# Four raw and four split buffers in place of six and three, in a split-precision adjacency matmul

## What is computed

```python
h = maximum(layernorm(x, axis=-1), 0.0)          # x: 8192 x 128, f32
x = x + (1.0 - 0.1) * (adj @ h) + 0.1 * h0       # adj: 8192 x 8192, f32; h0: 8192 x 128
```

## Time and profile before

| | |
|---|---|
| median of 3 runs | 709.2 us (709.12 to 709.41) |
| profiled execution, its own time | 709.23 us |
| its span in the trace | 707.4 us |
| PE busy | 702.4 us, 99% |
| DVE busy | 636.1 us, 90% |
| ACT busy | 531.6 us, 75% |
| bytes moved | 285.75 MB, mean 404 GB/s |
| chain that ended last | PE 99%, DMA 1% |

### The profile page before, as it was taken

How to read it: one execution, slowest core, us unless ns; L and a number is a source line. 1 busy time by engine, 2 the same in 40 slices (tenths; PEclk the granted TensorE clock), 3 DMA queues, 4 the chain that set the end, 5 groups by cost and what they waited for, 6 DMA issues and landing times.

```text
span 707.4 us, 8192 instructions
## 1 busy us (share of the span) xinstructions
PE 702.4 (99%) x3088; PEld 578.4 (82%) x3088; DVE 636.1 (90%) x567; ACT 531.6 (75%) x465; POOL 31.5 (4%) x38
## 2 busy tenths in 40 slices
PE   8999999999999999999999999999999999999998
PEld 5888888888888888888888888888888888888886
DVE  5999999999989999999998888888988898889885
ACT  5899988788788788778776767676767676767673
POOL 1101110000000000000000000000000000000000
PEclk9999999999999999999999999999999999999999
DMA  9999999999999999999999999999999999999990
GB/s 365 417 418 420 416 419 416 419 416 418 420 416 419 417 419 417 419 416 420 421 418 418 388 409 389 404 401 399 414 421 414 424 420 423 422 419 422 406 414 21
DMA packets 46551, 285.75 MB, mean 404 GB/s; under 512 B 5168, under 2 KB 9520, under 8 KB 14000
## 3 DMA queue, kind: packets, MB, share of 16 engines
q1 hardware_dynamic: 46080, 283.99, 98.0%
q10 hardware_dynamic: 432, 1.25, 0.5%
HBM read 281.02 MB, written 4.19 MB: 403 GB/s over the span
## 4 chain that ended last, share of the span: by engine, by line
PE 99%; DMA 1%; DVE 0%; SPq 0%; DVEq 0%; issue 0%
PE acc L478 16%; PE acc L473 16%; PE acc L474 16%; PE acc L462 16%; PE acc L451 16%; PE acc L457 16%; PE acc L420 1%; DMA raw<-early_dram 1%; PE acc L433 0%; PE acc L437 0%; PE acc L429 0%; DVE finished L368 0%; SPq L217 0%; DVEq L138 0%; DVEq L367 0%
## 5 line engine op out<-in xcount | busy, mean ns | idle before, releaser
L349 DVE TENSOR_TENSOR a_lo<-raw,a_hi 128x2048 fp32r<-128x2048 f32 (+2 forms) x310 | 585.4, 1907 | 55.7 <-ACT a_hi L305 54.8
L305 ACT ACTIVATE a_hi<-raw 128x2048 fp32r<-128x2048 f32 (+1 forms) x370 | 498.9, 1378 | 159.8 <-PE acc L478 100.1
L473 PE MATMUL acc<-a_hi,h_hi 128*128 128x512 f32 x512 | 199.2, 389 | 0.0
L474 PE MATMUL acc<-a_hi,h_lo 128*128 128x512 f32 x512 | 199.2, 389 | 0.0
L451 PE MATMUL acc<-a_hi,h_hi 128*128 128x512 f32 x504 | 167.5, 389 | 0.0
L457 PE MATMUL acc<-a_hi,h_lo 128*128 128x512 f32 x504 | 167.5, 389 | 0.0
L478 PE MATMUL acc<-a_lo,h_hi 128*128 128x512 f32 x512 | 136.8, 389 | 0.0
L462 PE MATMUL acc<-a_lo,h_hi 128*128 128x512 f32 x504 | 134.7, 389 | 0.0
L473 PEld LDWEIGHTS acc<-a_hi,h_hi 128*128 128x128 f32 x512 | 96.1, 188 | 20.0
L478 PEld LDWEIGHTS acc<-a_lo,h_hi 128*128 128x128 f32 x512 | 96.1, 188 | 20.0
L474 PEld LDWEIGHTS acc<-a_hi,h_lo 128*128 128x128 f32 x512 | 96.1, 188 | 19.9
(11 more groups left out here) (21 smaller groups left out, 31.5 us busy)
## 6 DMA issues: line engine op xcount, KB each, us to landing
raw<-tall_dram SPq DMA_DIRECT2D x128, 1024.0 KB, 8.3
raw<-wide_dram SPq DMA_DIRECT2D x126, 1024.0 KB, 11.8
res_sb<-res_dram SPq DMA_DIRECT2D x16, 512.0 KB, 10.2
x_sb<-x_dram SPq DMA_DIRECT2D x30, 128.0 KB, 11.9
out_dram<-finished SPq DMA_DIRECT2D x15, 256.0 KB, 8.6
raw<-early_dram ACTq DMA_DIRECT2D x2, 512.0 KB, 6.6
raw<-early_dram SPq DMA_DIRECT2D x2, 512.0 KB, 6.2
out_dram<-finished SPq DMA_DIRECT2D x2, 128.0 KB, 1.8
```

The source lines that it names most:

```text
L305: nc.scalar.activation(a_hi[:, q % SPLIT_SLOTS, cols], raw[:, q % RAW_SLOTS, cols], ACT.Copy).then_inc(hi_ready, 1)
L349: nc.vector.tensor_tensor(a_lo[:, q % SPLIT_SLOTS, cols], raw[:, q % RAW_SLOTS, cols], a_hi[:, q % SPLIT_SLOTS, cols].bitcast(fp32), ALU.s ...
L473: nc.tensor.matmul(bank, h_hi[:, k, :], a_hi[:, slot, cols], start=(k == 0), stop=False)
L474: nc.tensor.matmul(bank, h_lo[:, k, :], a_hi[:, slot, cols], start=False, stop=False)
```

## The change

One line: the raw slots go from six to four, and the split slots (a_hi and a_lo each) from three to four.

```diff
-RAW_SLOTS, SPLIT_SLOTS = 6, 3
+RAW_SLOTS, SPLIT_SLOTS = 4, 4
```

## The result

The changed kernel takes 758.2 us, the median of six runs from 752.7 to 765.9, against 709.3 us before. The ratio is 1.068, 95% interval 1.065 to 1.071. The runs of before lie within 0.4 us of each other; these spread over 13, and the ratio leaves out the longest, over 1.5% above the shortest. The forecast was 719 us with a range of 709 to 745. The profiled execution took 755.9 us, its span 754.1.

What follows compares the result with a forecast made beforehand. PE was taken to bound the kernel, its pace kept only if loads land within 6.6 us; 8.4 us in the wide stage and 1.7 late in the tall one, 10.1 on 709.23, gave 719 us, range 709 to 745.

Steps and rivals of the forecast that it cites:

- The bound and the loop of the raw slot: PE bounds at 2.72 us a piece; a slot goes through load, a_hi, a_lo, SP, with 4.3 us behind the landing.
- The landing: Load of a whole piece with no queue: about 5.5 us against 6.6 allowed, so the loop closes at 9.8 of 10.88.
- The terms of the sum: Wide stage from piece 44: 8.4 us; tall from 490 us: 1.7; before 116 us and tall to 490: 0.
- the lumps of DVE: Wide stage: DVE's other work delays issues by 1.0 or 1.6 us, idling DMA engines 0.44 us per four pieces.
- residual loads: They take 1.25 us each, 0.06 a unit in the wide stage, and leave little spare DMA rate late in the tall stage.
- the spread between the 16 engines: Wide stage: the slowest DMA engine decides the landing; raises the loss per four pieces from 0.3 to 0.4 us.
- Rival 2: The landing is long by itself, 7.8 us, loop 12.1 us, 786 us in all; chance 0.08 for anything above 745.
- the fourth split slot: Lets ACT run a piece further ahead, removes its 100.1 us of waits on PE; at most 0.2 us to gain.
- the moved stores: Stores move by two pieces in place but not in time, behind the same low_a: cost 0.
- the loads of x: At least 10.88 us lie between issue and statistics, against landings of 6 to 7 us: cost 0.
- The start: Piece 4 goes out at about 10 us instead of 3, its data due near 13: cost 0, at most 2 us.
- The range: 709 to 745 us, from rival 1's no loss to a shortest landing of 6.8 us; leaves out rivals 2 and 3.

Runs made afterwards that it cites:

- nores4: Changed kernel (four raw, four split slots) with only the first residual loaded and used for all chunks: 756.1 us, ratio 1.067.
- even13: Changed kernel with 13 matmuls a piece and an added SP wait, the load of piece q waiting for PE's piece q - 5: 771.4 us.
- p13: Kernel before (six raw, three split slots) with one matmul done twice in each piece, 13 matmuls: 766.5 us, one run.
- even4: Changed kernel, 12 matmuls a piece, with an added SP wait, the load of piece q waiting for PE's piece q - 5: 757.4 us, ratio 1.070.
- even12h: Changed kernel with a thirteenth matmul of 256 columns a piece and SP's added wait for PE's piece q - 5: 749.4, 751.5, 763.8 and 769.4 us.
- r4s3: Kernel before with four raw slots instead of six, split slots left at three: 757.5 us, ratio 1.068.
- p13r4: Changed kernel (four raw, four split slots) with one matmul done twice in each piece, 13 matmuls, no added wait: 768.6 us.
- r3s4: Changed kernel with three raw slots instead of four, four split slots: 837.4 us, one run.
- p13r4s3: Four raw and three split slots, against the changed kernel's four and four, with 13 matmuls a piece: 772.1 us, one run.
- p14: Kernel before (six raw, three split slots) with two matmuls done twice in each piece, 14 matmuls: 824.0 us, one run.
- two4: Changed kernel with each piece loaded as two halves of 512 KB, both issued only when the whole slot is free: 777.4 us, ratio 1.096.

## Why the prediction was wrong

- **The bound and the loop of the raw slot** were read rightly: PE at 99%, 4.3 us behind a landing, 6.6 us allowed, and "everything hangs on whether the load lands within 6.6 us". The span after is that loop, 11.6 us a round.
- **The landing, "I take about 5.5 us", is the step that failed**, and with it "the loop then closes at 9.8 us of 10.88". It closed at 11.6, with landings of 7.2 to 7.3. As a floor 5.5 was even high (4.8 us with two slots). But what counts is the landing at the pace that PE needs. The earlier trace rows had that: 7.8 us at 399 GB/s, with issues 2.72 us apart, in a stretch where the slots did not bind, since ACT waited for PE. I took those 7.8 us for a queue that the slots let stand. In the wide stage that was right (12.0 to 9.1 us with five slots). In the tall stage it was not: from 380 to 460 us five slots at PE's pace still had 7.6.
- **The terms of the sum** were sized by the spare DMA rate and the lumps of DVE (its other work between two low_a steps): 8.4 us wide, 1.7 late, nothing before 116 us and nothing from 356 to 490. Measured are, in this order, 20.5, 17.2, 2.8 and 6.1 us. A round of 11.6 in place of 10.88 us, 0.72 more in 63 rounds, gives 45 us in all against the 46.7 between the profiled executions. That is a mean, and the closeness is in part luck, as the stages differ. That residual loads are not the cause, nores4 shows. The lumps it left in. They may have a part in the wide stage, where the stretch behind a landing is 4.6 us on average against 4.3 in the tall one, but without them, from 380 to 460 us, PE loses time too. The 0.1 us a unit for the spread between the 16 engines no run shows.
- **Rival 2**, with a chance of 0.08 above 745, had the sum that holds (landing plus 4.3 us, over four slots) and was too dear, 786 us for landings of 7.8. Its reason, a landing that is long by itself, does not hold: from 380 to 460 us it is 4.8 and 4.9 us with two and three slots, and 7.0 in the loop of four.
- **The rest of the landing** the prediction did not see. Evenly spaced loads at a pace of 2.95 us can land in 5.0 to 5.4 us (even13 and p13, 430 to 500 us); 4.8 + 4.3 would let the loop run at 2.3 us a piece. The loop can therefore neither run slowly and evenly, as it would then speed up, nor at PE's pace, where the landing is over 6.6 us. It ran in between, with ACT's starts 2.4 to 3.6 us apart and landings of 7.2. Shown is that one added wait, which evens the issues and holds them back, takes the 7.2 away at a pace of 2.95 us. That the loop keeps itself uneven in this way is argued from even4 and even12h.
- **No cost of the fourth split slot, of the moved stores and of the loads of x**: as predicted, r4s3 and the waits show none. The start cost 2.8 us to piece 39 in the profiled execution and 0.3 in that of r4s3, near the 0 to 2 us that were forecast.
- **The range** ended at 745 with bounds that took a landing of 6.8 us, the smallest of the earlier trace rows, as the worst case. Its median, 7.8, was the row to use.

Open is what in the DMA path makes a landing near 370 GB/s 2 us longer in the loop of four slots, and whether the uneven issues do it or the slots that are filled again at once.

## What to carry to other kernels

Before a ring of buffers is made smaller, take the landing from a stretch where the ring does not bind and the pace is the one to be kept, and add the time to the slot's return. If that is more than slots times pace, there is a loss, at most the difference in every round: here 786 us against 758 measured, since the landing shortens a little as the loop slows. A floor measured with few loads out does not help. If slots must go, shorten what follows the landing or give slots back in parts: with the same four slots that brought 758 us to 720. Here one raw slot of the six was free (709.2 us with five and three, 8 KB less in each partition), and the second cost 48 us.

## What the runs showed of the hardware

- Landings of a 1 MB load from one queue with four slots and 13 matmuls, 430 to 500 us: 5.0 us with issues every 2.95 us and held back to PE (even13, 368 GB/s), 7.2 us without that wait and with ACT's starts 2.5 to 3.8 us apart (p13r4, 374 GB/s).
- With three slots and starts 2.4 to 3.8 us apart it is 4.9 us at 352 GB/s (r3s4), with four slots and uneven starts 7.8 at 358 (p13r4s3).
- From 380 to 460 us, with six slots and issues at PE's pace: 4.9 us at 336 GB/s (p14), 5.0 at 364 (p13), 7.8 at 399 (before), far below the 430 GB/s that the start moved. The mean rate and the spacing are not all of it: p13 with the same even issues had 4.9 us from 440 to 480 and 6.7 from 480 to 520, at 372 and 368 GB/s, and from 116 to 200 us even12h, with four slots and even issues, had 6.0 us at 397 GB/s.
- A kernel whose loads fail to keep up can scatter: 13 us over six runs for the changed kernel, 20 us over four for the one that switches, but 1.5 us for two4. The kernel that PE paces spreads over 0.4 us.
- Loads of 512 KB with rows of 4 KB (half pieces) reached 413 GB/s at most in a slice, loads of 1 MB with rows of 8 KB 424 in the kernel before. Which of size and row makes it was not tested.
